# First experts' blocks: splits in pairs, takes on ScalarE, ranks inside the first layer; self-attention: stacks in memory order, scores ahead of the values

## The chip, the cores and the metric

The kernel runs on one core of one Trainium2 chip. The metric is the device time of one execution in microseconds, the median of the runs shown. The core's engines (TensorE = PE, VectorE = DVE, ScalarE = ACT, GpSimd = POOL, SyncE = SP) each work through their own instruction list in order and wait for one another on semaphores. SP issues nearly all DMAs; POOL issues the indirect ones.

## The reference, cut to what matters

x is (4, 256, 256), the context (4, 4096, 256). Six layers run in a row; this change touches the third, the fifth and the sixth.

```
x = x + L0_xattn(layernorm(x), ctx, ctx)
x = x + L0_attn(layernorm(x), ...)
x = x + L0_ffn(layernorm(x), ...)          # experts: 2 shared, 8 routed, top 2 of 8
x = x + L1_xattn(layernorm(x), ctx, mask)  # most of the time
x = x + L1_attn(layernorm(x), ...)         # self-attention with rotary embedding, MLP
x = x + L1_ffn(layernorm(x), ...)          # self-attention, 8 experts of 256x256
```

```
# L0_ffn, per expert e:  W1 (256, 1024), W2 (1024, 256)
h = gelu(rmsnorm(u) @ W1[e] + b1[e]);  y_e = h @ W2[e] + b2[e]
out = u + sum(shared y_e) + sum(gate * y_e over the two best routed experts)
# self-attention, twice: 16 heads of 16, 4 batches of 256 positions
attn = softmax(q @ k.T * 0.25);  out = attn @ v
```

## The kernel before, in words

**Numbers in two halves.** Float32 products are made of float16 parts: a value is split into a high part (a cast) and a low part (value minus high part), and three products high x high, low x high, high x low are summed in PSUM. In the expert layer ACT makes the weights' high parts (`weights_high`, L1645), DVE their low parts (`weights_low`, L1980). ACT applies gelu to a first-layer result (`hidden`, L1654) into one of four slots of `hid_f`; DVE splits it with a CAST (L2059) and a subtraction (L2061) in `hidden_parts`. A `settle` is a wait of DVE for its own earlier instructions.

**Experts.** Expert 0 of the program's jobs is the first shared one (1024 tokens), jobs 1 to 15 (`NBLK`) are blocks of 256 slots, each of one routed expert, and job 16 is the second shared expert. `hidden_product` (L1182) makes one 128-row piece of the hidden layer out of 6 matmuls: 16 pieces of 512 columns for a shared expert, 8 of 256 columns for a block. The results go to three banks in turn. `second_layer` (L1215) makes one tile of 128 tokens out of 24 matmuls of 256 columns, in four banks in turn. The matmul order for blocks q = 1 to 15 is: transposes of block q+1 (`turn_block`, L1256), first layer of q, second layer of q-1.

**Routing.** DVE chooses the experts amid the first shared expert's splits (`select_experts`). After all 16 pieces of that first layer PE runs `ranks()` (L1225 to L1231, small float32 products), which count the tokens ahead of each; DVE turns them into slots (`place_tokens`, from L2008). From there SP loads the routed experts' weights and POOL scatters the tokens into `x_slots` with 16 indirect DMAs (L2473). Two biases' products (`turn_gates`) come between the shared expert and the blocks.

**A block's outputs.** DVE's `take_block` (L2078) scales a tile from PSUM into `yb`. In DVE's order of round q come: low part of the next block's tokens (L2083), 8 splits, `weights_low` (4 instructions), take of tile 0 of block q-1, `weights_low` (4), take of tile 1. SP's order of round q: weights of q+2, first half; tokens of block q+2 (`load_block`, L800); store of block q-1 (`store_block`, L805), which waits for both takes; weights of q+1, second half. Each weight half is 1 MB. So each token load stands in SP's queue behind the store of three blocks before.

**Self-attention.** For each of eight jobs PE projects queries or keys (L1377), and the result is split into `hi` and `lo`; SP stores both to DRAM (`self_scr`, L928) and loads them back (L938) as stacks: per head of 16 rows, high, low and high again lie in partition groups 0-15, 16-31, 32-47, and the same at 64 for every other head. A half of the batches needs 12 loads of 16 partitions. PE multiplies the values (`values`, L1386; 8 tiles, copied by DVE, L2242). Then comes a first pass: PE makes scores into a ring of two PSUM pairs (L1408), DVE takes their row maxima (L2252); batches 0, 1 and two units of batch 2 run ahead, the rest beside the steps. The maxima are split into three parts, transposed and stored by SP as three more rows of the stacks (`max_rows`, L914), so that the second scores (L1440) come out shifted; ACT exponentiates them (L1719) and PE weighs the values (L1433).

## Time and profile before

| | |
|---|---|
| median of 3 runs | 1984.81 us (1984.15 to 1984.89) |
| profiled execution | 1984.79 us, its span 1983.0 us |
| busy: PE, DVE, ACT, POOL | 85%, 67%, 54%, 14% of the span |
| mean granted TensorE clock | 0.916 of 2.4 GHz |
| first shared expert and routing | about 530 to 614 us |
| 15 routed blocks | about 614 to 800 us |
| second shared expert | about 800 to 853 us |
| cross-attention with its start | about 853 to 1540 us |
| first self-attention, from its projections | 1558 to 1671 us |
| second self-attention, from its projections | 1758 to 1859 us |

How to read it: the page's busy shares are averages over these stretches, which have different limits, so each stretch is read by itself in the chain of waits (the work that ended last, in order of time) and in the engines' timelines. A timeline line gives start, duration, engine, line of the program, operation, and in brackets the idle time before it with what ended it. Durations of neighbours overlap where an engine pipelines; the pitch from start to start is what a sequence costs.

### The profile page before, as it was taken

The page shows a single profiled execution, that of the slowest core. Times are in us where ns is not written, and L with a number is a line of the kernel's source. Part 1 is how long each engine was busy: PE and PEld are TensorE (multiplying, and loading weights), DVE is VectorE, ACT ScalarE, POOL GpSimd, SP SyncE. Part 2 cuts the span into 40 slices and gives each one's busy share as a digit, 9 for nine tenths or more (in the row PEclk, how much of TensorE's full clock was granted, in tenths as well). Part 3 has the DMA queues.
Part 4 walks back from the last instruction along what each step waited for, and adds up shares of the span by engine and source line. Part 5 has one row for each costly group of instructions (what it writes and reads, how often), then busy time and mean ns, then how long its engine had stood idle before and what let it go on. Part 6 is the DMA issues. An engine that isn't in the chain of part 4 may idle for free.

```text
span 1983.0 us, 34606 instructions
## 1 busy us (share of the span) xinstructions
PE 1692.6 (85%) x13836; PEld 918.5 (46%) x13836; DVE 1329.6 (67%) x2148; ACT 1066.6 (54%) x1898; POOL 275.3 (14%) x248
## 2 busy tenths in 40 slices
PE   6988868999689998856999999999999768986686
PEld 4566645666557887521333333333333334552342
DVE  4233344460457999549999999999981786239556
ACT  3312122878534776211999999999998015213410
POOL 3223013898130000300000000000000000000000
PEclk9999979999788999975999999999999879986878
DMA  8124012989433665256434434434200261044100
GB/s 315 64 85 123 1 43 59 298 277 306 145 117 126 216 214 181 75 96 94 82 59 81 93 59 79 95 59 78 63 25 2 44 71 45 1 76 56 44 0 21
DMA packets 144621, 196.61 MB, mean 99 GB/s; under 512 B 34422, under 2 KB 109832, under 8 KB 140200
## 3 DMA queue, kind: packets, MB, share of 16 engines
q1 hardware_dynamic: 142732, 190.07, 37.2%
q0 software_dynamic: 1728, 4.33, 0.7%
q8 instruction: 109, 1.79, 0.4%
q14 instruction: 52, 0.43, 0.1%
HBM read 143.04 MB, written 51.00 MB: 98 GB/s over the span
## 4 chain that ended last, share of the span: by engine, by line
DVE 43%; PE 40%; issue 5%; DMA 4%; POOL 3%; ACT 2%; SPq 1%; another core or an unknown queue 0%; DVEq 0%; ACTq 0%; POOLq 0%
DVE mx_part L2159 27%; DVE mx L2252 3%; PE pair L1543 3%; PE bank L1182 3%; PE pair L1215 3%; DVE w_lo L1980 2%; PE pair L1137 2%; PE bank L1035 2%; PE pair L1150 2%; DMA xT<-x_slots 2%; PE bank L1318 2%; PE bank L249 2%; PE pair L1377 2%; PE bank L1079 2%; POOL k_part L2459 2%
## 5 line engine op out<-in xcount | busy, mean ns | idle before, releaser
L1709 ACT ACTIVATE pexp_all<-bank 128x512 f32<-128x512 f32 x1024 | 551.8, 596 | 98.6 <-PE bank L1332 85.0
L2159 DVE TENSOR_REDUCE mx_part<-pair 128x2 f32<-128x1024 f32 x512 | 583.1, 1216 | 17.0 <-PE pair L1304 14.8
L1318 PE MATMUL bank<-pexp_all,vst 128*17 128x256 f32 x4096 | 321.7, 386 | 6.0 <-issue 6.0
L1304 PE MATMUL pair<-kst,qs 49*128 49x512 f16 x1024 | 210.0, 407 | 44.8 <-DVE mx_part L2159 28.0
L1332 PE MATMUL bank<-qs,kst 52*128 52x256 f16 x2048 | 203.2, 271 | 0.0
L1304 PEld LDWEIGHTS pair<-kst,qs 49*128 49x128 f16 x1024 | 50.4, 93 | 273.7 <-DVE mx_part L2159 215.1
L1332 PEld LDWEIGHTS bank<-qs,kst 52*128 52x128 f16 x2048 | 120.7, 95 | 57.0 <-ACT pexp_all L1709 18.4
L1719 ACT ACTIVATE pexp_all<-bank 128x512 f32<-128x512 f32 x128 | 67.6, 595 | 122.0 <-PE bank L1440 121.9
L1318 PEld LDWEIGHTS bank<-pexp_all,vst 128*17 128x17 f32 x4096 | 68.6, 95 | 114.7 <-issue 105.2
L1215 PE MATMUL pair<-w_hi,hid_hi 128*128 128x256 f16 x368 | 102.4, 278 | 8.2 <-issue 5.0
L1654 ACT ACTIVATE hid_f<-bank,b 128x256 f32<-128x256 f32 (+1 forms) x152 | 78.6, 518 | 52.0 <-PE bank L1182 35.1
L1215 PE MATMUL pair<-w_lo,hid_hi 128*128 128x256 f16 x368 | 102.4, 278 | 2.6 <-issue 2.6
L1215 PE MATMUL pair<-w_hi,hid_lo 128*128 128x256 f16 x368 | 102.3, 278 | 1.8 <-issue 1.8
L1980 DVE SCALAR_TENSOR_TENSOR w_lo<-w_f,w_hi 128x512 f16<-128x512 f32 x136 | 84.5, 685 | 6.3 <-ACT w_hi L1645 6.3
L2459 POOL TENSOR_TENSOR k_part<-k_f,k_part 128x512 f16<-128x512 f32 x64 | 83.5, 1323 | 34.9 <-ACT k_part L1615 34.6
L2495 POOL TENSOR_SCALAR neg_grp<-mx_grp 128x8 f32<-128x8 f32 x16 | 3.7, 233 | 607.4 <-DVE mx_grp L2179 607.4
L1645 ACT ACTIVATE w_hi<-w_f 128x512 f16<-128x512 f32 x136 | 73.2, 619 | 27.6 <-DMA b<-in_b_all 13.9
L238 ACT ACTIVATE deviation<-var_eps 128x8 f32<-128x8 f32 x11 | 2.3, 208 | 159.1 <-DVE var_eps L228 158.6
L1182 PE MATMUL bank<-xTs,w_hi 128*128 128x256 f16 x480 | 85.1, 284 | 0.0
L2432 POOL TENSOR_TENSOR ctx_lo<-ctx_sb,ctx_hi 128x2048 f16<-128x2048 f32 x16 | 62.8, 3946 | 146.5 <-ACT ctx_hi L1557 146.5
L2252 DVE TENSOR_REDUCE mx<-pair 128x4 f32<-128x1024 f32 x64 | 75.0, 1215 | 6.6 <-PE pair L1408 6.1
L2446 POOL TENSOR_TENSOR c_lo<-cT,c_hi 128x1024 f16<-128x1024 f32 x32 | 74.2, 2320 | 24.9 <-ACT c_hi L1597 24.9
(313 smaller groups left out, 2979.6 us busy)
## 6 DMA issues: line engine op xcount, KB each, us to landing
w_f<-in_w_all SPq DMA_DIRECT2D x34, 1024.0 KB, 5.8
kst<-k_scr SPq DMA_DIRECT2D x192, 128.0 KB
v_scr<-v_st SPq DMA_DIRECT2D x64, 272.0 KB, 3.3
vst<-v_scr SPq DMA_DIRECT2D x16, 1088.0 KB, 5.6
ctx_sb<-in_ctx SPq DMA_DIRECT2D x16, 1024.0 KB, 4.9
cT<-in_ctxT SPq DMA_DIRECT2D x32, 512.0 KB, 5.7
k_scr<-k_part SPq DMA_DIRECT2D x128, 128.0 KB, 3.6
x_slots<-zeros SPq DMA_DIRECT2D x1, 3840.0 KB, 21.2
```

Of the source, the lines that this page charges most:

```text
L1182: last = pe.matmul(bank[n % 3][:, 0:tk.stop - tk.start], w[:, piece, at:at + P], src[x_][:, k, tk], start=(k == 0 and x_ == 0 and w is w_h ...
L1215: last = pe.matmul(out_bank(n), hid_part[h_][:, m, at:at + P], w[:, WPIECES // 2 + m // 2, wc], start=(m == 0 and h_ == 0 and w is w_hi), ...
L1304: last = pe.matmul(pair[n % 2][:, e * 512:(e + 1) * 512], qs[g % NBK][rws, p, qt * P:(qt + 1) * P], kst[g % NBK][rws, p, kb * 512:(kb + 1) ...
L1318: last = pe.matmul(bank[3][32 * h:32 * h + HV, 0:S], vst[g % 2][:, c, h * HV:(h + 1) * HV], unit_exp[n % NUE][:, p * S:(p + 1) * S], start ...
L1332: return pe.matmul(bank[SCORE_BANKS[n % 3]][:, p * S:(p + 1) * S], kst[g % NBK][head_rows(e, X_MAX + 3), p, c * P:(c + 1) * P], qs[g % NBK ...
L1654: act.activation(hid_f[:, n % 4, 0:w], bank[n % 3][:, 0:w], ACT.Gelu, bias=b_1[q % 4][:, job % HM:job % HM + 1], scale=1.0 / W_SCALE).then ...
L1709: act.activation(unit_exp[n % NUE], bank[SCORE_BANKS[n % 3]], ACT.Exp, scale=SCALE).then_inc(s_exp, 1)
L1980: dve.scalar_tensor_tensor(out=w_part[1][q % 2][:, p_, :], in0=w_f[q % 2][:, p_, :], scalar=W_SCALE, in1=w_part[0][q % 2][:, p_, :], op0=A ...
L2159: dve.tensor_reduce(mx_part[:, :, 2 * p + qt, kb], pair[n % 2][:, :].rearrange("p (e k) -> p e k", e=2), X_AXIS, ALU.max).then_inc(s_mx, 1)
L2252: dve.tensor_reduce(dst, pair[n % 2][:, :].rearrange("p (e i k) -> p e i k", e=2, i=2), X_AXIS, ALU.max)\
L2446: pool.tensor_tensor(c_part[n % 2][1][:, :, :], cT[n % 3][:, :, :], c_part[n % 2][0][:, :, :], ALU.subtract).then_inc(s_clo, 1)
L2459: pool.tensor_tensor(k_[:, 1, :], k_f[job % 3][:, :], k_[:, 0, :], ALU.subtract).then_inc(s_klo, 1)
```

## The change

- `take_block` moves from DVE to ACT, into ACT's order between and behind the two `weights_high` of a round, and counts on a semaphore of its own, `s_yb`; `store_block` and the reuse of the four output banks wait on it for blocks.
- Block results are split two at a time: `block_hidden_parts` casts and subtracts 128x(2x256) where `hidden_parts` did 128x256 twice.
- `ranks()` runs after 9 of the first shared expert's 16 first-layer pieces, `place_tokens()` after 9 of its splits.
- `self_scr` gets the layout (query or key, high or low, half, 32 rows of a pair of heads, pair of heads, 512 positions), so that a row of a stack half is one run of 8 KB; the high and low copies that lie next to each other are loaded by one DMA of 32 partitions. A half takes 8 loads instead of 12. The stacks lie in the order of `stack_of`: the two batches of a half alternate. `max_rows` needs 6 DMAs a batch instead of 3.
- The values' copies move from DVE to ACT (`take_values`). PE multiplies `lead` tiles of values ahead of the first pass (0 in the first self-attention, 4 in the second) and one after each first-pass unit of batch 0 until all 8 are done.

```diff
-        self_scr = [dram(f"self_scr{i}", [2, 2, B, D, S], F16) for i in range(2)]
+        self_scr = [dram(f"self_scr{i}", [2, 2, 2, 2 * HD, H // 2, 2 * S], F16) for i in range(2)]
...
-        SELF_LOADS = 12
+        SELF_LOADS = 8
...
-        SELF_ROWS = 3 * 16
+        SELF_ROWS = 2 * 3 * 16
+        def stack_of(b, pair_):
+            return 2 * PAIRS_B * (b // 2) + 2 * pair_ + b % 2
...
-            sa5 = SelfAttention(0, sc)
+            sa5 = SelfAttention(0, sc, lead=0)
...
-            sa6 = SelfAttention(1, sc)
+            sa6 = SelfAttention(1, sc, lead=4)
...
+        RANK_JOB = HM + 1
...
             def store_block(q):
-                sp.wait_ge(s_acc, out_before(q) + out_tiles(q))
+                sp.wait_ge(s_yb, BLK // P * q)
...
-                        sp.dma_start(sa.q[at:at + HALF + 1:HALF, PAIRS_B * b:PAIRS_B * (b + 1), :],
-                                     m_prt[32 * b:32 * b + 32, i, :]).then_inc(signals["mrow"].s, 16)
+                        for qt in range(2):
+                            dst = sa.q[at:at + HALF + 1:HALF, stack_of(b, 0):stack_of(b, PAIRS_B - 1) + 1:2, qt * P:(qt + 1) * P]
+                            sp.dma_start(dst, m_prt[32 * b + qt:32 * b + 32:2, i, :]).then_inc(signals["mrow"].s, 16)
...
-                            sp.dma_start(scr[n, part, bs, m * P:(m + 1) * P, :].rearrange("b p q -> p b q"),
-                                         src[:, half, m, n * 512:(n + 1) * 512].rearrange("p (b q) -> p b q", b=2))\
+                            sp.dma_start(scr[n, part, half, :, 4 * m:4 * m + 4, :].rearrange("f h x -> h f x"),
+                                         src[:, half, m, n * 512:(n + 1) * 512])\
                                 .then_inc(signals["fst"].s, 16)
...
-                        order, dst = (((0, 1, 0), sa.q), ((0, 0, 1), sa.k))[n]
-                        for r, part in enumerate(order):
-                            for e in range(2):
-                                src = scr[n, part, bs].rearrange("b (h e d) q -> e d (b h) q", e=2, d=HD)[e]
-                                at = HALF * e + HD * r
-                                sp.dma_start(dst[at:at + HD, 2 * PAIRS_B * half:2 * PAIRS_B * (half + 1), :], src)\
-                                    .then_inc(signals[f"qk{half}_loaded"].s, 16)
+                        both, one, dst = ((0, 2, sa.q), (1, 0, sa.k))[n]
+                        for e in range(2):
+                            fs = slice(HD * e, HD * (e + 1))
+                            at = HALF * e + HD * both
+                            sp.dma_start(dst[at:at + 2 * HD, 2 * PAIRS_B * half:2 * PAIRS_B * (half + 1), :],
+                                         scr[n, :, half, fs].rearrange("s f h x -> s f (h x)"))\
+                                .then_inc(signals[f"qk{half}_loaded"].s, 16)
+                            at = HALF * e + HD * one
+                            sp.dma_start(dst[at:at + HD, 2 * PAIRS_B * half:2 * PAIRS_B * (half + 1), :],
+                                         scr[n, 0, half, fs]).then_inc(signals[f"qk{half}_loaded"].s, 16)
...
                 for job in range(hidden_jobs(q)):
+                    if q == 0 and job == RANK_JOB:
+                        ranks()
                     hidden_product(q, job)
...
             first_layer(0)
-            ranks()
             second_layer(0)
...
-                values(range(0, T))
+                values(range(sa.lead))
                 sa.wait(pe, "flo", len(SELF_JOBS))
                 for b in range(2):
                     for i in range(SELF_UNITS):
                         first_pass(b, i)
+                        if b == 0 and sa.lead + i < T:
+                            values([sa.lead + i])
...
+            def take_block(q, s_):          # ScalarE; VectorE's of the same name goes
+                n = out_before(q) + s_
+                act.wait_ge(s_w2, n + 1)
+                if q >= 3 and s_ == 0:
+                    act.wait_ge(s_ys[q % 2], 16 * ((q - 1) // 2))
+                act.activation(yb[q % 2][:, s_, :], bank[4 + n % 4][:, 0:D], ACT.Copy, scale=1.0 / W_SCALE).then_inc(s_yb, 1)
...
                 hidden(q)
                 if q >= 2:
                     weights_high(q + 1, 0)
+                    take_block(q - 1, 0)
                     weights_high(q, 1)
+                    take_block(q - 1, 1)
+            for s_ in range(BLK // P):
+                take_block(NBLK, s_)
             weights_high(JOBS - 1, 1)
...
+            def block_hidden_parts(q):
+                ts = slice((q % 2) * BLK, (q % 2 + 1) * BLK)
+                for m in range(0, HM, 2):
+                    n = hidden_before(q) + m
+                    src = hid_f[:, n % 4:n % 4 + 2, 0:BLK]
+                    dve.wait_ge(s_gelu, n + 2)
+                    st.link(dve.tensor_copy(hid_part[0][:, m:m + 2, ts], src))
+                    st.settle()
+                    dve.tensor_tensor(hid_part[1][:, m:m + 2, ts], src, hid_part[0][:, m:m + 2, ts], ALU.subtract)\
+                        .then_inc(s_hlo, 2)
...
-            hidden_parts(0, range(4, 2 * HM))
+            hidden_parts(0, range(4, RANK_JOB))
             place_tokens()
+            hidden_parts(0, range(RANK_JOB, 2 * HM))
```

## Rows read from the trace of the kernel before

**Rows 1.** Page, part 4: the chain of work that ended last, by engine.

```profile
DVE 43%; PE 40%; issue 5%; DMA 4%; POOL 3%; ACT 2%; SPq 1%; another core or an unknown queue 0%; DVEq 0%; ACTq 0%; POOLq 0%
```

**Rows 2.** Timeline of PE in the blocks: start, us, engine, line, shapes, [idle].

```profile
646.09 0.66 PE L1256 MATMUL bank<-ident,xT 128*128 128x128 f32 x4 [1.99 <-DMA xT<-x_slots]
...
671.47 0.66 PE L1256 MATMUL bank<-ident,xT 128*128 128x128 f32 x4 [1.66 <-DMA xT<-x_slots]
...
682.33 0.27 PE L1215 MATMUL pair<-w_hi,hid_lo 128*128 128x256 f16 x1
...
695.08 0.66 PE L1256 MATMUL bank<-ident,xT 128*128 128x128 f32 x4 [1.15 <-DMA xT<-x_slots]
...
768.63 0.66 PE L1256 MATMUL bank<-ident,xT 128*128 128x128 f32 x4 [0.51 <-DMA xT<-x_slots]
```

**Rows 3.** Waits from 640 to 785 us: total, times, longest.

```profile
PE bank L1256 <- DMA xT<-x_slots: 10.3, 9, 2.0
```

**Rows 4.** Timeline of SP's DMA issues in the blocks: the stores.

```profile
635.31 0.37 SPq L805 DMA_DIRECT2D y_slots<-xT  x1
...
684.72 0.37 SPq L805 DMA_DIRECT2D y_slots<-xT  x1
```

**Rows 5.** Timeline of DVE: splits at 256 and at 512 wide.

```profile
552.84 0.42 DVE L2059 CAST hid_hi<-hid_f 128x512 f16<-128x512 f32 x1
...
553.90 0.42 DVE L2059 CAST hid_hi<-hid_f 128x512 f16<-128x512 f32 x1
...
673.82 0.28 DVE L2059 CAST hid_hi<-hid_f 128x256 f16<-128x256 f32 x1
...
674.48 0.29 DVE L2059 CAST hid_hi<-hid_f 128x256 f16<-128x256 f32 x1
```

**Rows 6.** Groups by shape, 646 to 769 us: busy, mean ns, idle before.

```profile
L1980 DVE SCALAR_TENSOR_TENSOR w_lo<-w_f,w_hi 128x512 f16<-128x512 f32 x80 | 49.9, 685 | 0.0
...
L1654 ACT ACTIVATE hid_f<-bank,b 128x256 f32<-128x256 f32 x80 | 37.9, 474 | 15.1 <-PE bank L1182 11.7 <-DVE hid_lo L2061 2.5
...
L2078 DVE TENSOR_SCALAR xT<-pair 128x256 f32<-128x256 f32 x20 | 8.4, 419 | 0.0
```

**Rows 7.** Timelines of PE, DVE and SP in both self-attentions.

```profile
1591.98 7.13 PE L1386 MATMUL bank<-wb,xT 128*128 128x256 f32 x24 [2.02 <-DVE self_v L2242]
...
1599.50 11.40 DVE L2252 TENSOR_REDUCE mx<-pair 128x4 f32<-128x1024 f32 x10
...
1771.78 2.79 SPq L938 DMA_DIRECT2D self_q<-self_scr  x6
...
1776.87 5.45 PE L1386 MATMUL bank<-wb,xT 128*128 128x256 f32 x24 [0.17 <-DVE self_v L2242]
...
1787.28 1.04 PE L1408 MATMUL pair<-self_k,self_q 48*128 48x256 f16 x8 [4.95 <-DMA self_k<-self_scr]
```

**Rows 8.** Timelines of ACT and PE at the last routed block.

```profile
790.19 2.19 ACT L1645 ACTIVATE w_hi<-w_f 128x512 f16<-128x512 f32 x4 [2.60 <-DMA w_f<-in_w_all]
...
793.41 0.35 PE L1215 MATMUL pair<-w_hi,hid_hi 128*128 128x256 f16 x1 [3.16 <-DVE w_lo L1980]
```

**Rows 9.** Timelines of POOL's scatter and of PE's second block.

```profile
589.36 0.97 POOL L2473 DMA_INDIRECT x_slots<-tok,slots  x1 [0.30 <-issue]
...
613.55 1.09 PE L1256 MATMUL bank<-ident,xT 128*128 128x128 f32 x4 [1.93 <-DVE xTs L2083]
```

**Rows 10.** Windows: us, engines busy (x count), PE clock, DMA share, GB/s.

```profile
671.00:695.00 24.00, 22.27 (x200) 19.55 (x200) 22.46 (x57) 17.45 (x36) 0.00 (x0) 1.00 0.64 220
...
574.00:577.60 3.60, 3.60 (x35) 3.23 (x34) 0.42 (x1) 2.19 (x4) 2.90 (x3) 1.00 0.99 332
...
577.60:591.50 13.90, 4.82 (x22) 1.97 (x21) 0.00 (x0) 4.37 (x8) 9.69 (x10) 0.65 0.60 217
...
860.00:862.00 2.00, 1.42 (x7) 0.56 1.03 131
...
1782.00:1784.00 2.00, 0.32 (x2) 1.00 1.28 117
```

More of the change, by code:

```diff
@@ L576, in build, with __init__ @@
         class SelfAttention:
-            def __init__(self, turn, scope):
+            def __init__(self, turn, scope, lead):
                 i = f"self{turn}_"
-                self.turn = turn
+                self.turn, self.lead = turn, lead
                 self.hi = sb(i + "hi", [P, 2, KT, NTOK], F16, scope)
@@ L922, in self_io @@
                 for half in range(2):
-                    bs = slice(2 * half, 2 * half + 2)
                     for i in range(4):
@@ L1198, in out_bank_free @@
             def out_bank_free(n):
-                if n >= 4:
-                    pe.wait_ge(s_acc, n - 3)
+                last = n - 4
+                blocks = out_before(1), out_before(JOBS - 1)
+                if last >= blocks[1]:
+                    pe.wait_ge(s_acc, last + 1 - (blocks[1] - blocks[0]))
+                elif last >= blocks[0]:
+                    pe.wait_ge(s_yb, last + 1 - blocks[0])
+                elif last >= 0:
+                    pe.wait_ge(s_acc, last + 1)
             def second_layer(q):
@@ L1711, in _, with take_values @@
             act_turn(act, turn3o)
+            def take_values(sa):
+                for t in range(T):
+                    sa.wait(act, "vproj", t + 1)
+                    act.activation(sa.v[:, t, :, 0:HD], bank[2 + t % 2][:, 0:D].rearrange("p (h d) -> p h d", d=HD), ACT.Copy)\
+                        .then_inc(signals["vtaken"].s, 1)
             def self_exp(sa):
@@ L1724, in _ @@
             act_turn(act, turn4)
+            take_values(sa5)
             self_exp(sa5)
@@ L2053, in hidden_parts @@
                     half, m = divmod(job, HM)
-                    if shared(q):
-                        at, w = half * 512, 512
-                    else:
-                        at, w = (q % 2) * BLK, BLK
+                    ts = slice(half * 512, (half + 1) * 512)
                     dve.wait_ge(s_gelu, n + 1)
-                    st.link(dve.tensor_copy(hid_part[0][:, m, at:at + w], hid_f[:, n % 4, 0:w]))
+                    st.link(dve.tensor_copy(hid_part[0][:, m, ts], hid_f[:, n % 4, :]))
                     st.settle()
-                    dve.tensor_tensor(hid_part[1][:, m, at:at + w], hid_f[:, n % 4, 0:w], hid_part[0][:, m, at:at + w],
-                                      ALU.subtract).then_inc(s_hlo, 1)
+                    dve.tensor_tensor(hid_part[1][:, m, ts], hid_f[:, n % 4, :], hid_part[0][:, m, ts], ALU.subtract)\
+                        .then_inc(s_hlo, 1)
+            def block_hidden_parts(q):
[8 more added lines that the diff above has]
+                        .then_inc(s_hlo, 2)
             def out_of(n):
@@ L2071, in take_shared @@
                                          op0=ALU.mult, op1=ALU.add).then_inc(s_acc, 1)
-            def take_block(q, s_):
-                n = out_before(q) + s_
-                dve.wait_ge(s_w2, n + 1)
-                if q >= 3 and s_ == 0:
-                    dve.wait_ge(s_ys[q % 2], 16 * ((q - 1) // 2))
-                dve.tensor_scalar(yb[q % 2][:, s_, :], out_of(n), 1.0 / W_SCALE, None, ALU.mult).then_inc(s_acc, 1)
             def block_low(q):
@@ L2117, in _ @@
                     block_low(q + 1)
-                hidden_parts(q, range(HM))
+                block_hidden_parts(q)
                 if q >= 2:
                     weights_low((q + 1, 0))
-                    take_block(q - 1, 0)
                     weights_low((q, 1))
-                    take_block(q - 1, 1)
-            for s_ in range(BLK // P):
-                take_block(NBLK, s_)
             weights_low((JOBS - 1, 1))
@@ L2238, in self_attention @@
             def self_attention(sa, take_projection):
-                def take_values(tiles):
-                    for t in tiles:
-                        sa.wait(dve, "vproj", t + 1)
-                        dve.tensor_copy(sa.v[:, t, :, 0:HD], bank[2 + t % 2][:, 0:D].rearrange("p (h d) -> p h d", d=HD))\
-                            .then_inc(signals["vtaken"].s, 1)
                 ring = Ring()
@@ L2273, in self_attention @@
                     take_projection(job)
-                take_values(range(0, T))
                 for b in range(2):
```

10 lines of the change are left out of this document (7 added, 3 removed).

## The prediction

> **What bounds the kernel now.** I read the page's chain of waits first: DVE holds 43% of it and PE 40% [rows 1], most of it in cross-attention, which this change leaves alone. Then I asked the chain, the waits and each engine's timeline for the three stretches that the diff touches.
>
> Routed blocks (about 620 to 793 us). PE does one round per block: four transposes (L1256), eight first-layer jobs, two second-layer tiles. From the transposes at 671.47 to the last matmul at 682.33, plus its 0.11 pitch, that is 10.97 us of work [rows 2]. Yet the ten rounds from 646.09 to 768.63 take 12.25 us each [rows 2], and PE stands 10.3 us in nine waits for the block's tokens [rows 3]. The tokens are late because of one loop: PE ends a round at 682.44, DVE's take_block comes behind its weights_low, SP issues the store at 684.72 (2.28 us later; 1.8 to 2.5 over the rounds), and behind it in SP's order two 1 MB weight loads and the token load, with which PE starts at 695.08, 10.36 us after the store [rows 2, 4]. Nine such trips take 9.95 to 11.4 us, mean 10.8; two are in the rows. The tokens of that load belong to the round after next, so two rounds last 10.97 + 2.2 + 10.8 = 24.0, or 12.0 each. The rest of the 12.25 is the clock: two of the ten rounds, those beginning at 646.09 and 731.33, ran partly at 1.2 GHz after a wait of about 2 us and took 12.64. DVE has no reserve either: eight splits of 0.66 us from start to start [rows 5], eight weights_low of 0.60 (0.69 each, overlapping), two takes of 0.34 and 0.8 for the next block's low part [rows 6] are 11.6 us a round.
>
> Self-attention, twice. In the first PE projects, multiplies the values until 1599.1 (half of it at 1.2 GHz) and only then does DVE start its maxima, 1.13 us a piece [rows 7]. In the second PE is done with the values at 1782.3 and stands 4.95 us until the stacks have landed [rows 7]: the loads, issued from 1771.78, need 15.4 us.
>
> **The change part by part.**
>
> *Takes of block outputs to ACT.* Removes 2 x 0.33 us from DVE a round and puts 2 x 0.47 on ACT, by the nearest row, ACT's 128x256 gelu from PSUM [rows 6] (bounds 0.4 to 0.6). ACT has 8.4 gelu and token copies' 0.84, 4.3 of weights_high and now 0.9, under 10 of 11 us. In its order it is through gelu at 6.4 us after the round's start, through the first weights_high at 8.5; PE's first tile is ready at 8.5; the second weights_high ends at 11.1; PE's second tile is ready at 11.15. So neither take waits long, and what stands behind them (the next block_high) waits for PE's next transposes anyway. The store goes out 0.2 + 0.47 = 0.65 us after PE's round instead of 2.2. Two rounds: 10.97 + 0.65 + 10.8 = 22.4, 11.2 each, against PE's 10.97.
>
> *Split two at a time.* A pair at 512 wide costs 1.06 us from start to start against 2 x 0.66 at 256 wide [rows 5]: 1.06 us a round less. With the takes DVE falls from 11.6 to 9.9 us. It no longer sets the round, but it is nearly full: last pair ready at 6.4, done 7.5, eight low parts to 12.3, next block_low wanted at 12.7. hid_f comes free in pairs, pair 0 at 3.6 us, and gelu 4 asks for it at 3.9: no stall. If that cover were gone, the 0.3 us would recur each round.
>
> Sum for the blocks: first token wait ends at 633.02 (round's end) + 11.45 = 644.5 instead of 646.09, 1.6 us; ten rounds give 1.05 each, 10.5 (the waits fall below 0.5 us, so I let the two clock drops go with them); at the end w_f for the last block is late: ACT starts on it at 790.19, PE's second layer stands 3.16 us until 793.41 [rows 8]. That store is issued at 781.88, again behind the take; 1.6 us earlier here too. Together 13.7; I take 13.5. Bounds: 4 (store earlier, but the trip grows by as much, only the clock drops saved) and 15.5 (the 48 matmuls after the 3.16 us wait keep the 2.4 GHz, 1.8 more).
>
> *Ranks after nine jobs.* ranks() costs PE 3.5 us in either place (562.59 to 566.08). place_tokens starts at 558.2 rather than 566.3, POOL's 16 scatters and the three weight loads 8 us earlier. What is behind place_tokens on DVE, seven parts of 1.06, ends at 570.0; second_layer(0) needs them from its fifth tile, not before 576. PE can run six to seven jobs ahead on three banks and four hid_f slots, 8 us against DVE's absence of 4.5. But nobody waits for the scatter: its last instruction starts at 589.36, and PE wants the tokens after the b2 products, at 610.5, the second block's transposes starting at 613.55 [rows 9]. From 577.6 to 591.5 PE got only 22 matmuls through [rows 10] (idle "issue", nothing it waits for), while POOL issued the scatter; that stall moves to about 570 to 584 and stays inside second_layer(0), as long. Value 0, bounds -2 (first-layer matmuls of 512 columns need fewer instructions a us) and +6 (the stall begins as soon as POOL does).
>
> *Scores ahead of the values, copies on ACT, first self-attention (lead 0).* PE's idle time from 1588.25 to 1591.6 stays (last split), then comes the first pair at once. Pairs and values alternate: 0.23 + 0.86 us at 2.4 GHz, 0.43 + 1.71 at 1.2. DVE takes 1.13 a piece, so at the high clock the values are hidden, at the low one not. PE enters after 3.4 us of idleness; after the 2 us idle of before, it took 3.6 us of work until the high clock came back. So two units at the low clock: DVE's first eight maxima end at 1602.9, not 1599.5 + 9.0 = 1608.5. Gain 5.6, with the stacks landing at 1591.3 (below); I take 5.3. Bounds 0 (low clock all through: 8 x 2.14) and 8.
>
> *Stacks in memory order.* Loads per half go from 12 of 16 rows x 16 pieces of 512 B to 4 of 32 rows and 4 of 16 rows, 8 KB in one piece, still 1.57 MB. SP saves 4 x 0.45 us of issuing. How fast do they move? 16 rows in 512 B pieces go at 117 GB/s with all queues busy (1782 to 1784) [rows 10]: 13.4 us. The kst loads of cross-attention, 16 rows in 4 KB pieces, go at 131 [rows 10]: longer pieces alone give 12.0 us. Weights into 128 rows move at 332 [rows 10]: 4.7 us. No row shows 32 rows. I take the mean of the ends, 9.3 us, which is also near what the 16-row part at 131 and the 32-row part at twice that would give (8.0). The Trainium skill, page "SBUF — State Buffer", section "Door 1: The DMA port swizzle (why `[64,N]` ≈ `[32,N]`)", says that a transfer's rate goes by the ports its partitions reach, four for 16 rows and eight for 32. By that page's 104 and 189 GB/s the sum, an estimate, would be 10.6 us; our 16-row rows agree with its four ports, and no row here tests its eight.
>
> Second self-attention (lead 4): landed at 1771.8 + 2 + 9.3 = 1783.1 instead of 1787.1; four tiles of values are done by 1778.3, the other four are alternated. PE waits 4.8 us again and enters at the low clock: two units stretched, 1.5 us lost on DVE. Gain 4.8 - 1.5 = 3.3. Bounds 0 (landing as late as 1786) and 8 (landing at 1778.6, clock kept). The later half's stores are no longer held in SP's queue; its loads land near 1800, wanted at 1804.
>
> *Maxima rows, 3 to 6 DMAs a batch.* 0.51 us each on SP, so 1.5 more; in both layers batch 0 has 8.5 us from its split to the first scores and needs 5.3, later ones have 10. Nothing, unless that cover shrinks by 3.
>
> Sum: 13.5 + 0 + 5.3 + 3.3 = 22.1. The profiled execution is 1984.79 us (span 1983.0 and 1.8 around it), the median 1984.81: 1962.7.
>
> **The rivals.**
> - *The trip grows.* The store is earlier, but the 2.5 MB behind it move no sooner. For it: in the rows the trip varies from 9.95 to 11.4. Against: over two rounds the DMA engines are busy 0.64 of the time [rows 10], with their idle part ahead of each store. Blocks give 4: 1972.
> - *Rows, not pieces, set the load.* 32 rows are no faster than 16: the first stack lands at 1593.5 and 1785.8; self-attention gives 3.5 + 0: 1968.
> - *Clock and loads both kind.* Full rate, high clock: 15.5 + 2 + 8 + 7: 1952.
> - *Slower: the weight load closes a loop through ACT.* ACT's second take stands behind weights_high(q,1), which waits for the w_f load issued behind the previous store. Loop: 1.1 (issue) + landing + 2.19 + 0.47. With the 7.2 us of 782.99 to 790.19 it is 11.0 and harmless; from a landing of 8.5 us it exceeds 12.25 and every round is slower. At 10 us, 13.8 a round: 1.5 x 13 more, less 8.6 of self-attention: 1996. Against it: in the steady rounds ACT never waited for w_f by more than 1.3 us.
>
> **How the numbers follow.** Forecast 50%, the trip grows 17%, rows set the load 15%, both kind 9%, slower 5%, a mixture that ends within 0.2% 4%. 0.2% (4 us) is about what a measurement of this kernel can tell from no change. The forecast's own range is 1958 to 1967; with the neighbours 1953 to 1974. Faster 0.91, same 0.04, slower 0.05.
>
> **What would show it.** Rounds of 11.2 us at L1256 and stores 0.7 us after each round's last matmul; token waits under 0.5 us and a granted clock of 1.0 from 644 on. CAST and subtraction at 128x512, four a round. Second layer of the first expert ending still near 601. First L2252 near 1592 and 1783. Wrong if rounds stay at 12, if ACT waits for w_f ahead of the takes, if PE's "issue" stall grows with the earlier scatter, or if L2252 starts after 1786.

## The result: 2031 us, 2.3% slower

| | us, median | lowest to highest | runs |
|---|---|---|---|
| before | 1984.85 | 1984.15 to 1989.17 | 4 |
| changed | 2031.33 | 2027.63 to 2034.89 | 4 |

The ratio is 1.0229, its 95% interval 1.0202 to 1.0257. The forecast was 1962.7, with a range of 1953 to 1974. The profiled execution took 2034.18 us, its span is 2032.4.

First the chain of waits by engine, against [rows 1]: transfers, and SyncE's own queue, have come in where DVE lost share.

```profile
PE 43%; DVE 36%; DMA 6%; issue 5%; SPq 4%; POOL 4%; ACT 2%; another core or an unknown queue 0%; DVEq 0%; ACTq 0%; POOLq 0%
```

I cut both executions at marks which both programs have, the first or last instruction of a line, read from each line's own view. Four of the marks are in these rows: first and last transposes, first maxima, first product with the last layer's experts. A row has line, engine, operation, count, shortest/median/longest ns, first and last start, forms. First those of before, then those of the changed kernel:

```profile
L1256 PE MATMUL bank<-ident,xT x60: 272/273/474, 610.5 to 769.0; 128*128 128x128 f32 x60
L2252 DVE TENSOR_REDUCE mx<-pair x64: 1202/1215/1226, 1599.5 to 1833.3; 128x4 f32<-128x1024 f32 x64
L1543 PE MATMUL pair<-l_we,xT x128: 592/592/1222, 1909.3 to 1965.7; 128*128 128x512 f32 x128
```

```profile
L1274 PE MATMUL bank<-ident,xT x60: 272/273/473, 613.2 to 760.4; 128*128 128x128 f32 x60
L2285 DVE TENSOR_REDUCE mx<-pair x64: 1202/1224/1226, 1597.1 to 1882.7; 128x4 f32<-128x1024 f32 x64
L1564 PE MATMUL pair<-l_we,xT x128: 592/592/1222, 1958.6 to 2015.1; 128*128 128x512 f32 x128
```

| stretch | before | changed | difference | forecast |
|---|---|---|---|---|
| start of the program to first expert's first layer (code untouched) | 539.5 | 546.4 | +6.9 | 0 |
| to first block's transposes (ranks) | 71.0 | 66.8 | -4.2 | 0 |
| first to last block's transposes | 158.5 | 147.2 | -11.3 | -12.1 |
| to the first maxima of cross-attention | 114.9 | 111.2 | -3.7 | -1.6 |
| cross-attention, to the first projection | 674.0 | 674.1 | +0.1 | 0 |
| first self-attention: projection to first maxima | 41.6 | 51.4 | +9.8 | |
| ... and to the router after it | 93.4 | 111.1 | +17.7 | (both) -5.3 |
| to the second's last projection | 81.5 | 81.5 | 0 | 0 |
| second self-attention, to the first product with the last layer's experts | 134.9 | 168.9 | +34.0 | -3.3 |

The rows add up to 49.3, the two spans differ by 49.4; the kernel's end behind the last mark takes as long in both. The blocks did about what was forecast. The two self-attentions lost 61.5 us where 8.6 were to be won. There PE stands four times for its stacks. First PE's timeline of the changed kernel at those places (start, us, engine, line, shapes, [idle before, and what ended it]), then SP's issues of the first loads and of the stores behind them:

```profile
1596.48 0.61 PE L1425 MATMUL pair<-self_k,self_q 48*128 48x256 f16 x4 [20.34 <-DMA self_k<-self_scr]
...
1633.50 1.03 PE L1425 MATMUL pair<-self_k,self_q 48*128 48x256 f16 x8 [14.74 <-DMA self_k<-self_scr]
...
1819.31 0.61 PE L1425 MATMUL pair<-self_k,self_q 48*128 48x256 f16 x4 [25.59 <-DMA self_k<-self_scr]
...
1856.08 1.03 PE L1425 MATMUL pair<-self_k,self_q 48*128 48x256 f16 x8 [14.40 <-DMA self_k<-self_scr]
```

```profile
1570.10 0.68 SPq L943 DMA_DIRECT2D self_q<-self_scr  x1
...
1574.73 0.56 SPq L934 DMA_DIRECT2D self_scr<-self_hi  x1
1575.33 7.78 SPq L934 DMA_DIRECT2D self_scr<-self_lo  x1
1583.15 9.35 SPq L934 DMA_DIRECT2D self_scr<-self_hi  x1
1592.54 1.71 SPq L934 DMA_DIRECT2D self_scr<-self_lo  x1
```

From the first load's issue at 1570.10 to the scores at 1596.48 are 26.4 us, and SP itself is held 7.78 and 9.35 us in the issue of a store. One would look for a crowded queue. The windows say the reverse: the columns are those of [rows 10], the last three being PE clock, share of the 16 DMA engines that is busy, and GB/s.

```profile
1586.00:1596.00 10.00, 0.00 (x0) 0.00 (x0) 0.00 (x0) 0.00 (x0) 0.00 (x0) 0.50 0.16 62
```

In the ten microseconds in which everybody waits for these loads, 0.16 x 16 = 2.5 DMA engines are busy. In the kernel before all were (1.28 at 1782 to 1784 [rows 10], more than 16 packets in flight at once). That gave the theory. As the programs are compiled, the load of high and low part together reads with counts 2 x 16 x 4096 and writes 32 x 4096; the store reads 128 x 512 and writes 4 x 32 x 512; all transfers of the stacks before have 16 or 128 outermost on both sides. **Few engines**: a transfer is spread over as many of the 16 engines as divides both outermost counts, so these run on 2 and 4. The trace bears it out in one more way: each engine closes its part of a transfer with a packet of 4 bytes, and over the eight stores of the first half there are 128 such packets before (16 a store) and 32 in the changed kernel (4 a store). The Trainium skill, page "DMA: Bandwidth & Descriptors", section "Why a DMA increments its semaphore by 16 and not by 1", has this rule: the largest number up to 16 that divides the slowest dimension on both sides, and on SyncE's queue always the lowest-numbered engines. The counts of closing packets agree with it; which engines they are, no row here can show.

The packets themselves, each with its start and length in the trace, say it most directly. While the second half lands in the changed kernel (1610 to 1633 us), exactly two packets are in flight for 20.4 of the 23 us. While the first half's stores run (1555 to 1570) it is four for 9.0 of the 15 us, and five, where neighbours overlap, for 2.8.

The rivals were **long pieces or few rows** (pieces of 8 KB into 16 or 32 partitions are slow by themselves; the prediction had the part on rows as a rival), and **the order** (scores between values, copies on ACT).

### The profile page after: what moved, and what is told of

Same layout as the page of the kernel before. It is cut to its first block, busy times and chain, and to the rows that moved or that the text cites. A ratio compares the mean times of both kernels' runs of the same rounds, so it can differ in the third digit from the quotient of the medians.

```text
span 2032.4 us, 34554 instructions
## 1 busy us (share of the span) xinstructions
PE 1697.5 (84%) x13836; PEld 923.1 (45%) x13836; DVE 1306.3 (64%) x1982; ACT 1083.6 (53%) x1944; POOL 276.1 (14%) x248
## 4 chain that ended last, share of the span: by engine, by line
PE 43%; DVE 36%; DMA 6%; issue 5%; SPq 4%; POOL 4%; ACT 2%; another core or an unknown queue 0%; DVEq 0%; ACTq 0%; POOLq 0%
DVE mx_part L2198 26%; PE bank L1191 5%; PE pair L1233 5%; PE pair L1564 3%; SPq L934 2%; DMA self_k<-self_scr 2%; PE bank L1044 2%; PE pair L1146 2%; PE pair L1159 2%; PE bank L249 2%; PE bank L1335 2%; POOL k_part L2491 2%; PE bank L1088 2%; DMA xT<-x_slots 2%; PE bank L307 1%
## 5 line engine op out<-in xcount | busy, mean ns | idle before, releaser
L1675 ACT ACTIVATE hid_f<-bank,b 128x256 f32<-128x256 f32 (+1 forms) x152 | 78.6, 519 | 51.4 <-PE bank L1191 38.2
L1425 PE MATMUL pair<-self_k,self_q 48*128 48x256 f16 x256 | 30.9, 333 | 89.0 <-DMA self_k<-self_scr 75.1
L238 ACT ACTIVATE deviation<-var_eps 128x8 f32<-128x8 f32 x11 | 2.3, 208 | 159.0 <-DVE var_eps L228 158.5
L1578 ACT ACTIVATE ctx_hi<-ctx_sb 128x2048 f16<-128x2048 f32 x16 | 29.9, 1905 | 94.3 <-PE bank L991 86.9
```

The lines of the kernel that those rows point to most:

```text
L1675: act.activation(hid_f[:, n % 4, 0:w], bank[n % 3][:, 0:w], ACT.Gelu, bias=b_1[q % 4][:, job % HM:job % HM + 1], scale=1.0 / W_SCALE).then ...
```

## The experiments

Kernels that are compared by ratio had runs of the kernel before beside them on the same chip. The chips differ: before took 1963.3, 1960.5 and 1988.3 us in the three sets of runs. So the ratios and the lengths of stretches are to be compared, not the times.

**Loads of 16 rows, 8 KB pieces kept.**

```diff
-SELF_LOADS = 8
+SELF_LOADS = 12
-    sp.dma_start(dst[at:at + 2 * HD, ...], scr[n, :, half, fs].rearrange("s f h x -> s f (h x)"))
-    ...                                                              # and the one of 16 rows
+    for at, part in ((both, 0), (both + 1, 1), (one, 0)):
+        at = HALF * e + HD * at
+        sp.dma_start(dst[at:at + HD, ...], scr[n, part, half, fs])
```

> The changed kernel with each load of a high and low part together (outermost count 2 at its source, 32 rows of 8 KB) issued as two of 16 rows of 8 KB; memory order and stores unchanged. Theory 'few engines' (a transfer runs on as many of the 16 DMA engines as divides the outermost count on both sides: 2 for these loads, 4 for the stores): the stacks land 10 to 12 us after their issue instead of 25, in all four halves; both self-attentions lose their four waits of 15 to 26 us; some 1969 us (before 1985, less 12 for the blocks, less 3). Rival 'long pieces into few rows are slow': pieces are still 8 KB and rows fewer, so landings stay at 25 us or grow; 2031 or more. Rival 'order of scores and values': 2031, stacks wait as before.

1966.22 us, ratio 1.0015 (0.9999 to 1.003). The loads land 14.4 us after their issue instead of 26.4, with the same bytes, the same 8 KB pieces and half the rows. "Long pieces" is out, and so is "the order" as cause of the loss. Sixteen or more packets are in flight for 7.0 of the 9 us from 1561 to 1570. The ratio came 1% short of the forecast. Waits of 8.38, 13.72 and 3.34 us for the stacks were left: the stores still have 4 outermost, and the order costs too (both below).

**The old stacks.** Memory order, stores, loads and rows of maxima as before; all else as changed.

> The changed kernel with the stacks' memory order, stores, loads and rows of maxima of the kernel before; split of blocks, takes on ACT, ranks, scores ahead of the values and the copies on ACT kept. Theories 'few engines' and 'long pieces' alike: the whole loss is in the transfers, so 1985 - 12.2 (blocks, as read from the trace after) - 5 (first self-attention's order) - 0 = 1968, range 1964 to 1973. Rival 'order of scores and values' (the alternation or the copies on ACT lose it): both self-attentions stay long, over 2000.

1959.78 us, 0.9987 (0.9967 to 1.0006): 2.5 us faster than before where 17 were expected. The blocks kept their gain, 146.2 us from first to last transposes. But the self-attentions took 38.1 + 100.1 and 141.8 us, against 135.0 and 134.9 before: 10 us longer, with exactly the old transfers. So the order, or the copies on ACT that came with it, is not free either; the run with values first, below, keeps the copies and parts the two.

**Head pair, row, column in memory**: a store is one block of 128 KB, a load 16 rows of eight 1 KB pieces, 12 loads a half as in the first experiment.

```diff
-self_scr: [2, 2, 2, 2 * HD, H // 2, 2 * S]
+self_scr: [2, 2, 2, H // 2, 2 * HD, 2 * S]
-    scr[n, part, half, :, 4 * m:4 * m + 4, :].rearrange("f h x -> h f x")        # store, 4 outermost
+    scr[n, part, half, 4 * m:4 * m + 4].rearrange("h f x -> (h f) x")            # 128 outermost
+    scr[n, part, half, :, fs].rearrange("h f x -> f h x")                        # load, 16 outermost
```

> The changed kernel with the stacks in memory as head pair, row, column: each store is one contiguous 128 KB over 128 rows, each load 16 rows of eight 1 KB pieces, outermost counts 128 and 16 on both sides; 12 loads a half. 'Few engines': all transfers on 16 engines; half-0 stores no longer late (first load issued 2.5 us earlier than in the changed kernel), landing 10 to 12 us after issue, 1966 us (3 less than the form with 8 KB pieces, whose stores stay on 4 engines). 'Long pieces': 1 KB pieces at 16 rows land in 12 to 13 us, also some 1968; it parts from 'few engines' only by the first run of this call. 'Order': over 2000.

1955.89 us, 0.996 (0.9943 to 0.9977), where 1966 of 1985 would have been 0.990: what is missing is about what the order lost in the run before. 16 closing packets a store; the first load is issued 1.8 us after the last store, not 4.2. Landing takes 14.4 us, as with 8 KB pieces, and 15.5 with the old 512 B: the length of the pieces is worth about 1 us.

**High and low part side by side**, so that 32 rows are loaded with 32 outermost.

```diff
+self_scr: [2, 2, H // 2, 2, 2, HD, 2 * S]          # n, half, head pair, e, part, d, x
+    scr[n, half, 4 * m:4 * m + 4, :, part].rearrange("h e d x -> (h e) d x")     # store, 8 outermost
+    scr[n, half, :, e].rearrange("h s d x -> (s d) h x")                         # load, 32 outermost
```

> The changed kernel with high and low part next to each other in memory, so that their load is 32 rows with outermost count 32 on both sides (eight 1 KB pieces a row), 8 loads a half as in the changed kernel; stores with outermost counts 8 and 128, thus 8 engines. 'Few engines': loads on 16 engines; tells whether 32 rows take data faster than 16: landing after 8 us instead of 12 if they do, 1962 us; 1968 if rows don't matter. 'Long pieces' or 'few rows': no better than the form with 16 rows. 'Order': over 2000.

1953.31 us, 0.9952 (0.9936 to 0.9968), again short of the forecast (0.988). Landing after 12.5 us instead of 14.4, not after 8; 8 closing packets a store. The window in which these loads run, and behind it one of the form with 16 rows:

```profile
1551.00:1558.00 7.00, 2.44 (x6) 0.76 (x4) 5.49 (x9) 0.00 (x0) 0.00 (x0) 0.96 1.06 150
```

```profile
1554.00:1561.00 7.00, 4.20 (x10) 1.44 (x8) 6.33 (x11) 0.00 (x0) 0.00 (x0) 1.00 1.17 125
```

So loads of which half have 32 rows take data faster than loads of 16 rows alone (150 GB/s against 125), as the prediction assumed for its 9.3 us; the assumption was right and beside the point, since the changed kernel's 32-row load never had the engines. The prediction's estimate by the Trainium skill, page "SBUF — State Buffer", section "Door 1: The DMA port swizzle (why `[64,N]` ≈ `[32,N]`)", was 10.6 us; 12.5 less the 2 us that it put ahead of the transfer are 10.5, so this run agrees with the sum. It agrees less with the parts: the form with 16 rows alone moved the same 1.57 MB in 12.4 us (14.4 less 2), where 104 GB/s would make it 15.1, an estimate.

**The kernel before once more, with a profile.**

> The kernel before, once more with a profile, because the chip of the last call ran it in 1963 us, 21.5 us less than the first did. Theory 'an effect of the chip': the 21 us are gone from stages in which PE had idle time for which the profile names no wait (577.6 to 591.5 us, during the scatter, and 814 to 828, during the gather), about 10 us in each. Rival 'a general factor': every stage is 1.1% shorter.

1959.82 us. The first row is while POOL issues the scatter (in [rows 10] the same stretch had 22 matmuls). The second is the whole of POOL's gather, and the third the whole gather in the first profile of before:

```profile
577.60:591.50 13.90, 13.29 (x123) 11.67 (x121) 5.24 (x12) 6.57 (x12) 10.84 (x11) 1.00 0.75 265
...
789.40:809.30 19.90, 19.90 (x106) 10.05 (x105) 19.39 (x33) 11.70 (x17) 15.31 (x16) 1.00 0.34 100
```

```profile
803.90:824.70 20.80, 16.36 (x75) 6.85 (x72) 12.76 (x23) 6.87 (x10) 16.22 (x16) 1.00 0.34 96
```

On this chip PE isn't starved during scatter and gather, that is, it doesn't stand there without a wait that the profile shows. (The expectation's 814 to 828 us is not the gather here: POOL was done with it at 809.3.) From the first expert's first layer to the first transposes it takes 56.2 us instead of 71.0, from the last transposes to cross-attention 102.3 instead of 114.9; the blocks (157.4), cross-attention and the self-attentions (41.6, 93.4, 134.6) are the same to 1.1 us. So the 24.9 us between the two spans are 27.4 from these two places and 1.8 from the others, less 4.2 that the start took longer.

**Without the edits of the blocks**, from the form with parts side by side: takes on DVE, splits one at a time.

> The form with high and low part next to each other (1953 us, ratio 0.9952), with the takes of block outputs back on DVE and the splits one at a time. By the prediction's 13.5 us and the 11.3 us that the changed kernel's first profile shows between first and last transposes of the blocks, this is 11 to 13.5 us slower than that form: ratio 1.001 to 1.003. Rival 'an effect of the chip': if the chip's own 21 us came out of the same waits, the edit is worth under 4 us and the ratio stays under 0.998.

1965.55 us, 1.0013 (0.9995 to 1.0032): 12 us slower than that form by the medians' ratios to their own runs of before, 0.6%. First to last transposes 154.8 us, against 145.3 in that form: 9.5. The two runs were on two chips; on this one, the two forms below that have the block edits took 146.3 and 148.3, so the edits gave 6.5 to 8.5 us there.

**Only the pairs kept**, takes on DVE, again from the form with parts side by side.

```diff
-    act.activation(yb[...], bank[4 + n % 4][:, 0:D], ACT.Copy, scale=1.0 / W_SCALE).then_inc(s_yb, 1)
+    dve.tensor_scalar(yb[...], out_of(n), 1.0 / W_SCALE, None, ALU.mult).then_inc(s_acc, 1)
```

> The form with high and low part next to each other (ratio 0.9952), pairs still split two at a time, but the takes of block outputs back on DVE behind weights_low. Between first and last transposes of the blocks it had 145.3 us, and 154.8 with neither edit. By the prediction the take's move brings the store forward by 1.5 us a round (8 to 9 us of the ten) and the pairs only keep DVE from being the bound: 152 to 154 here. Rival 'DVE's 11.6 us a round was the bound': most comes from the pairs, 147 to 149.

1984.93 us, 0.9986 (0.9966 to 1.0006), and 157.5 us from first to last transposes, against 159.3 in another profile on this chip whose blocks are as before (the stacks alone, below) and 146.9 in the changed kernel's: the pairs alone gain 1.8 us at the most, and both expectations (152 to 154, 147 to 149) were missed. Profiles of one and the same block code differ by as much (157.4 and 154.8 on the chip of the runs above). The changed kernel's DVE and ACT show why:

```profile
650.41 0.43 DVE L2108 CAST hid_hi<-hid_f 128x512 f16<-128x512 f32 x1
650.94 0.69 DVE L2110 TENSOR_TENSOR hid_lo<-hid_f,hid_hi 128x512 f16<-128x512 f32 x1
651.72 0.43 DVE L2108 CAST hid_hi<-hid_f 128x512 f16<-128x512 f32 x1
```

```profile
650.55 0.47 ACT L1675 ACTIVATE hid_f<-bank,b 128x256 f32<-128x256 f32 x1 [0.18 <-PE bank L1191]
651.21 0.47 ACT L1675 ACTIVATE hid_f<-bank,b 128x256 f32<-128x256 f32 x1 [0.18 <-PE bank L1191]
```

DVE starts a pair every 1.31 us, and two single splits are 2 x 0.66 = 1.32 [rows 5]. That pitch isn't DVE's own. ACT waits 0.18 us ahead of each gelu for PE, whose piece of 6 matmuls takes 6 x 0.109 = 0.65 us, so two pieces are ready every 1.31 us. The second gelu ends at 651.68, the pair's CAST starts at 651.72. A cheaper split only waits for the next piece: from a round's transposes to the first `weights_low` it is 7.58 us in the changed kernel (646.59 to 654.17), 7.66 before (671.47 to 679.13).

**Ranks back behind the first layer**, from the form with parts side by side.

> The same form with the ranks back behind the whole first layer and place_tokens behind all splits. In the first pair of profiles the blocks' first transposes moved 2.7 us later with the ranks early (610.5 to 613.2). Theory 'early ranks cost': 2 to 3 us faster than the form it comes from, ratio 0.994. Rival 'nobody waits for them': no difference, 0.9952; that they gain: over 0.9965.

1954.42 us, 0.9958 (0.9941 to 0.9975), against 0.9952: no difference, 57.5 us to the first transposes with either. This chip was one without the starvation. Where it shows, late ranks took 71.0 and 71.5 us to the first transposes, early ones 66.8, 68.9, 68.4 and 63.2: the -4.2 of the result is probably a gain of early ranks on such a chip, though four profiles that spread over 5.7 us don't size it.

**Values first again**, in both self-attentions, from the same form.

```diff
-sa5 = SelfAttention(0, sc, lead=0)
+sa5 = SelfAttention(0, sc, lead=8)
-sa6 = SelfAttention(1, sc, lead=4)
+sa6 = SelfAttention(1, sc, lead=8)
```

> The same form with all eight tiles of values ahead of the first scores in both self-attentions, as in the kernel before, the copies still on ACT. PE waits 5.1 and 7.4 us for the stacks in the form it comes from, and values would fill that: first self-attention 8 tiles take 6.9 us at 2.4 GHz, so scores begin 2 us later, less what the kept clock gives; second: four more tiles, 3.4 us, inside the wait of 7.4. Theory 'order gains': 5.3 us slower in the first, 0 in the second, ratio 0.9979. Rival 'the wait is paid either way': within 2 us of 0.9952.

1951.9 us, 0.9944 (0.9923 to 0.9965). That is the lowest ratio here, but its interval overlaps that of the form it comes from (0.9952), as the rival of the expectation had it. The profiles' stretches tell more, and they say faster, where 5.3 us slower was expected: 37.6 + 93.6 = 131.2 us against 36.1 + 99.2 = 135.3 in the first self-attention, 135.0 against 138.0 in the second. The run without early ranks, on the same chip as this one, has 135.2 and 138.0. PE's timelines with scores first and with values first, where the first scores begin:

```profile
1558.53 0.61 PE L1424 MATMUL pair<-self_k,self_q 48*128 48x256 f16 x4 [5.09 <-DMA self_k<-self_scr]
1559.08 2.07 PE L1402 MATMUL bank<-wb,xT 128*128 128x256 f32 x4
1561.08 0.61 PE L1424 MATMUL pair<-self_k,self_q 48*128 48x256 f16 x4
...
1565.56 1.13 PE L1402 MATMUL bank<-wb,xT 128*128 128x256 f32 x4
1566.62 0.39 PE L1424 MATMUL pair<-self_k,self_q 48*128 48x256 f16 x4
1566.95 1.13 PE L1402 MATMUL bank<-wb,xT 128*128 128x256 f32 x4
1568.01 0.39 PE L1424 MATMUL pair<-self_k,self_q 48*128 48x256 f16 x4
```

```profile
1561.86 7.07 PE L1402 MATMUL bank<-wb,xT 128*128 128x256 f32 x32
1568.86 0.61 PE L1424 MATMUL pair<-self_k,self_q 48*128 48x256 f16 x8
```

A unit and a tile of values take 2.55 us at 1.2 GHz (1558.53 to 1561.08) and 1.39 at 2.4 (1566.62 to 1568.01). DVE wants a unit every 1.13. So DVE is kept waiting for each unit that follows a tile (1.32 us twice, then 0.16 or 0.17), the first two tiles whole at the low clock, in which PE came out of its 5.09 us of idleness. Values first have no idleness before them, run at the high clock, and fill the wait for the stacks.

**The changed kernel once more.** A chip on which before takes 1960 us was expected; the one used was like the first.

> The changed kernel once more, beside the runs of before on this call's chip, where before takes some 1960 us. If the loss is in the self-attentions' waits for their stacks, which no other experiment's chip changed, it stays in microseconds: first scores 51 us after the projections began (41.6 before), the second self-attention 34 us longer; blocks 11 us less. Sum +47 us less 11: near 2005 us, ratio 1.02 to 1.027. Rival 'the early stages of the first chip': a ratio outside it.

2032.84 us beside 1988.32, ratio 1.0229 (1.0193 to 1.0265). Self-attentions 51.4 + 111.0 and 169.0 us, blocks 146.9: the same stretches as in the first profile. Whether the loss keeps its size on a chip of 1960 us, this run can't say.

**The stacks alone**, on the kernel before: memory order, stores, loads and rows of maxima of the change.

> The kernel before with nothing changed but the stacks: their memory order, stores of outermost count 4, loads of outermost count 2 with 32 rows and 16 with 16 rows, six DMAs for each batch's maxima. 'Few engines' has the whole loss here: each half lands 24 to 26 us after its issue. Values are first here, so they fill 7 us of the first wait: self-attentions 23 us (first) and 30 us (second) longer than before; ratio 1.025 to 1.03. Rival 'the order of scores and values has a part in the loss of the changed kernel': under 1.02.

2055.8 us, 1.0334 (1.0293 to 1.0375). 51.5 + 110.8 and 171.4 us in the self-attentions: 27.3 and 36.5 longer than before, without any change in the order of scores and values. This edit alone costs more than the whole change, because the block edits are not there to pay. I had taken 23 and 30 us, and a ratio of at most 1.03.

**Stores on four engines, loads on sixteen**: the form head pair, row, column with one unused row behind each head pair.

```diff
-self_scr: [2, 2, 2, H // 2, 2 * HD, 2 * S]
+self_scr: [2, 2, 2, H // 2, 2 * HD + 1, 2 * S]
-    scr[n, part, half, 4 * m:4 * m + 4].rearrange("h f x -> (h f) x")
+    scr[n, part, half, 4 * m:4 * m + 4, 0:2 * HD]                                # 4 outermost
```

> The form in order head pair, row, column (1956 us, ratio 0.996), with one unused row of 1 KB behind each head pair, so that a store's 128 pieces of 1 KB are no longer one block and its outermost count at the destination is 4 instead of 128; loads as they were. 'Few engines': 4 closing packets a store instead of 16; the first load goes out 4 us after the half's last store instead of 1.8, the second half's stores queue up on SP, the first scores come 2 to 3 us later in the first and up to 7 in the second self-attention: ratio 0.998 to 1.001. Rival 'only the loads matter': 0.996.

1985.01 us, 0.9987 (0.9966 to 1.0008). Nothing but a gap in memory has been added: same bytes, rows, pieces, order. The closing packets fall from 16 to 4 a store, and PE waits 8.91 and 14.08 us for its stacks instead of 5.79 and 7.30:

```profile
1581.16 0.61 PE L1422 MATMUL pair<-self_k,self_q 48*128 48x256 f16 x4 [8.91 <-DMA self_k<-self_scr]
...
1779.93 0.61 PE L1422 MATMUL pair<-self_k,self_q 48*128 48x256 f16 x4 [14.08 <-DMA self_k<-self_scr]
```

```profile
1563.99 0.61 PE L1422 MATMUL pair<-self_k,self_q 48*128 48x256 f16 x4 [5.79 <-DMA self_k<-self_scr]
...
1755.80 0.61 PE L1422 MATMUL pair<-self_k,self_q 48*128 48x256 f16 x4 [7.30 <-DMA self_k<-self_scr]
```

That is the cleanest proof of "few engines", for stores. The two forms ran on different chips, but the first experiment, with stores of 4 outermost on the chip of the second pair of lines, has nearly the same waits (8.38 and 13.72 us). The paired loads were not varied in their outermost count alone; there it stands on the first experiment, on the 2.5 busy engines and the two packets in flight, and on the form with 32 outermost, which lands the same 32 rows in half the time.

## Why the prediction was wrong

**Stacks in memory order: the step that failed.** It gave the load 9.3 us, between 4.7 (weights into 128 rows) and 13.4 (16 rows in 512 B pieces), on the ground that rows and pieces set the rate. The measured value, 24 us and more, lay outside both ends, since a third thing sets it that no row of before varied: how many engines a transfer gets. All transfers there had 16. The bounds "from the nearest rows" were rows of another kind. Replacing 12 loads by 8 looked like 4 x 0.45 us saved; the landing took 26.4 to 26.5 us in all four halves, 11 more than the 15.5 to 15.9 of the old transfers where PE waited for them (15.5 in before, 15.6 and 15.9 in the run with the old stacks). The stores, cut from 16 engines to 4, cost the rest. Issued first, they delayed the first load (4.2 us behind the last store's issue instead of 2.0, in the second self-attention 7.5 instead of 2.0). Those of the second half held SP for 17 us while the paired loads ran, with two or four packets in flight for 17.9 of the 20 us from 1576 to 1596, so they seem to have shared the loads' engines; PE's second wait (14.7 and 14.4 us) is new as well. An estimate of the size: if two engines carry the paired loads, each has 16 packets of 8 KB from each of the four and one from each of the four others. At 0.31 (the median) to 0.39 us (the mean of the half) a packet, 68 of them take 21 to 27 us; from the first to the last of these packets it was 24.2 (1571.57 to 1595.77).

Three slips in the working did not matter beside this. The mean of 4.7 and 13.4 is 9.05, not 9.3. ACT's gelu is 3.8 us a round [rows 6], not 8.4, and only with 3.8 is the sum under 10. The second self-attention's gain counts PE's wait of 4.8, where the landing came 4.0 earlier, so 2.5 and not 3.3. And 117 and 131 GB/s for 16 rows lie 12 and 26% above the 104 with which they were said to agree.

**Rival "rows set the load"** (1968 us) pointed at the right transfer with too small a price; **"the trip grows"** is partly true (below); the slower rival, w_f closing a loop through ACT, did not occur: no wait of ACT for w_f shows between 640 and 762, and PE had these token waits:

```profile
PE bank L1274 <- DMA xT<-x_slots: 3.6, 4, 1.6
```

**Takes on ACT: right**, though the token waits did not fall below 0.5 us each. Eleven rounds from 635.20 to 760.05 took 124.85 us, before 135.61 (633.02 to 768.63): 10.8 gained, 12.1 forecast; the late weights at the last block made 1.40 us of PE's 3.16. The stores leave some 0.65 us after the last matmul, as forecast (658.17 against 657.45 + 0.11); PE's and SP's timelines:

```profile
657.45 0.27 PE L1233 MATMUL pair<-w_hi,hid_lo 128*128 128x256 f16 x1
...
670.21 0.66 PE L1274 MATMUL bank<-ident,xT 128*128 128x128 f32 x4 [1.57 <-DMA xT<-x_slots]
```

```profile
658.17 0.37 SPq L811 DMA_DIRECT2D y_slots<-xT  x1
```

The trip behind this store is 12.04 us (658.17 to 670.21), and the other three on which PE waited 10.8, 11.7 and 11.3, where 10.8 was taken: the mean round is 11.35, not 11.2. The clock stayed at 2.4 GHz (granted 1.00 from 640 to 762), as forecast. Without the take's move it is 157.5 us: all but some 1.8 us of the gain is its.

**Pairs: wrong.** 1.06 us was read from a stage in which pieces lay ready. In the blocks PE's pace sets 1.31 for a pair, as it does for two single splits, so no time of a round is saved; that DVE no longer sets the round rests on the takes' 0.7 us.

**Ranks: value 0**, measured -4.2 here, outside the bounds (-2 to 6), and 0 on a chip without starvation. The mechanism that I bounded upwards went the other way.

**Scores ahead of values: wrong in sign.** The step "pairs and values alternate, 0.23 + 0.86 us at 2.4 GHz" was mis-sized: it is 1.39 (a tile 1.06, a pair of scores 0.33), which is more than DVE's 1.13, so the values were not hidden at either clock. Eight tiles in a row take 7.00 us, 0.88 each; what the alternation itself adds no row of before showed. With the old stacks the two self-attentions lost 3.2 and 6.9 us where 5.3 and 3.3 were to be won. The waiting PE did enter them at 1.2 GHz for two units, as the prediction said.

**Rows of maxima: right.** Where the stacks landed in time, 24 short DMAs lie within 42 us on SP (parts side by side), 12 within 40 (old stacks), and in no form does a wait on them show.

## What to carry to other kernels

Before changing an access pattern, write down the outermost count on both sides as the compiled instruction has it: merging two transfers into one, or reordering so that pieces become long, can leave 2 or 4 outermost, and then 2 or 4 of 16 engines work. The sign in a profile is a long wait for DMA beside a low share of busy DMA engines. Fill a wait for a transfer with work that needs no other engine, rather than interleaving that work later with a stage that another engine paces; and before you count on an operation's shorter pitch, see whether it is the engine's own or that of what feeds it.

## What the runs showed of the hardware

- A gap of one row in memory (contiguous 128 x 512 to 4 x 32 x 512) took a store from 16 engines to 4: closing packets of 4 bytes, 16 and 4. With loads of 2 outermost, two packets were in flight for 20.4 of 23 us.
- With two packets in flight, 8 KB took 0.31 us, the median (second half of the changed kernel); with 16 engines writing into 16 rows the same packet took 0.96 us, the mean (first experiment), 137 GB/s in sum as an estimate. The form with 32 rows in half its loads reached 150 GB/s, that with 16 rows alone 125.
- PE's starvation while POOL issues indirect transfers comes and goes with the chip: 22 matmuls in 13.9 us in one profile, 123 in another of the same program on another chip. In the gather PE was busy 16.4 of 20.8 us in the one, 19.9 of 19.9 in the other. The two stretches that hold them differ by 27 us of 1985. Its cause stays open.
- The untouched first 540 us varied by 10 us (539.5 to 549.9) between profiles; this also is unexplained, and is why the stretches are compared and not the spans.
